# Expert routing weights spread over partitions by DMA instead of by TensorE

## The reference

```python
E, K = (16, 4); I_MOE, I_SH = (176, 704)
h = hidden_states.reshape(-1, 256)                  # 1024 tokens
probs = softmax(h @ router_w.T)                     # 16 experts
top_vals, top_idx = top_k(probs, K)
top_vals = top_vals / maximum(top_vals.sum(-1), 1e-9)
comb = zeros((N, E)).at[arange(N)[:, None], top_idx].add(top_vals)
g = einsum('nh,ehi->eni', h, w_gate)
u = einsum('nh,ehi->eni', h, w_up)
y = einsum('eni,eih->enh', silu(g) * u, w_down)
routed = einsum('enh,ne->nh', y, comb)
shared = silu(h @ sh_gate) * (h @ sh_up) @ sh_down
sg = sigmoid(h @ sh_gate_w)
return routed + sg * shared
```

## Time and profile before

| | |
|---|---|
| time, median of 3 runs | 1107.69 us (1105.7 to 1107.95) |
| profiled execution | 1106.63 us, of which the span from first to last instruction is 1104.8 |
| TensorE, matmul | 957.0 us busy, 87% |
| VectorE | 774.9 us, 70% |
| ScalarE | 644.1 us, 58% |
| GpSimd | 505.3 us, 46% |
| DMA | 43.12 MB moved |
| TensorE's clock, mean granted | 0.953 of full |
| share of the chain that ended last | TensorE 60%, VectorE 21%, ScalarE 8%, issue 8%, GpSimd 2% |

### The profile page before, as it was taken

How to read it: one execution, slowest core, us unless ns; L and a number is a source line. 1 busy time by engine, 2 the same in 40 slices (tenths; PEclk the granted TensorE clock), 3 DMA queues, 4 the chain that set the end, 5 groups by cost and what they waited for, 6 DMA issues and landing times.

```text
span 1104.8 us, 15499 instructions
## 1 busy us (share of the span) xinstructions
PE 957.0 (87%) x5250; PEld 597.8 (54%) x5250; DVE 774.9 (70%) x1292; ACT 644.1 (58%) x1517; POOL 505.3 (46%) x392
## 2 busy tenths in 40 slices
PE   5899797664767757789989999999999999999998
PEld 3666543241222225566667777777675655555555
DVE  4578789898999987788888777778875453233222
ACT  2655488888898628667886777777662332111110
POOL 3222364542878514787777566677554322000000
PEclk8899799896999988899999999999999999999999
DMA  9734014000000000000000620000040000000000
GB/s 334 300 132 153 1 45 134 2 1 0 1 0 0 1 0 1 1 1 2 1 1 1 186 75 3 2 1 1 1 134 1 1 1 1 1 20 1 0 1 20
DMA packets 24270, 43.12 MB, mean 39 GB/s; under 512 B 3648, under 2 KB 19968, under 8 KB 22656
## 3 DMA queue, kind: packets, MB, share of 16 engines
q1 hardware_dynamic: 24192, 42.14, 11.2%
HBM read 41.08 MB, written 1.05 MB: 38 GB/s over the span
## 4 chain that ended last, share of the span: by engine, by line
PE 60%; DVE 21%; ACT 8%; issue 8%; POOL 2%; DMA 0%; DVEq 0%; ACTq 0%; SPq 0%; POOLq 0%
PE ps L2336 14%; PE ps L2357 9%; PE ps L1908 4%; PE ps L1921 4%; DVE arena L1112 4%; PE ps L1867 4%; PE ps L1875 3%; DVE ps L1108 3%; ACT ps L2181 3%; PE ps L1892 3%; PE ps L1900 2%; PE ps L1882 2%; DVE arena L1117 2%; PE ps L2346 2%; PE ps L445 2%
## 5 line engine op out<-in xcount | busy, mean ns | idle before, releaser
L2375 DVE TENSOR_TENSOR arena<-arena,ps 128x512 f32<-128x512 f32 (+1 forms) x56 | 38.5, 688 | 145.9 <-ACT arena L2368 143.8
L2368 ACT ACTIVATE arena<-ps,arena 128x512 f32<-128x512 f32 (+1 forms) x56 | 38.4, 686 | 156.0 <-PE ps L2336 156.0
L2260 POOL TENSOR_TENSOR arena<-arena 128x4 f32<-128x4 f32 x96 | 98.8, 1029 | 50.1 <-DVE arena L2032 47.5
L2357 PE MATMUL ps<-wide,arena 128*128 128x256 f32 (+1 forms) x448 | 106.3, 380 | 0.0
L2181 ACT ACTIVATE ps<-ps,arena 128x128 f32<-128x128 f32 x256 | 88.4, 355 | 28.5 <-DVE arena L2011 28.5
L2173 ACT ACTIVATE arena<-ps,ones 128x512 f32<-128x512 f32 x96 | 68.1, 786 | 61.2 <-PE ps L1882 61.2
L2357 PEld LDWEIGHTS ps<-wide,arena 128*128 128x128 f32 (+1 forms) x448 | 84.7, 190 | 17.9 <-issue 1.8
L2336 PE MATMUL ps<-XT,wide 128*128 128x512 f16 (+1 forms) x384 | 93.3, 379 | 0.0
L2011 DVE TENSOR_REDUCE arena<-ps 128x4 f32<-128x512 f32 x64 | 43.7, 689 | 53.2 <-PE ps L1892 53.1
L1875 PE MATMUL ps<-wide,arena 128*128 128x512 f16 x256 | 67.1, 398 | 13.6 <-ACT arena L2173 7.1
L1112 DVE TENSOR_TENSOR_SCAN arena<-arena,ps 128x1024 f32<-128x1024 f32 x32 | 73.2, 2287 | 1.1
(11 more groups left out here) (343 smaller groups left out, 2321.7 us busy)
## 6 DMA issues: line engine op xcount, KB each, us to landing
side<-in_wproj SPq DMA_DIRECT2D x4, 1024.0 KB, 5.5
wide<-in_w_down SPq DMA_DIRECT2D x1, 3584.0 KB, 13.9
side<-in_w_gate SPq DMA_DIRECT2D x1, 3520.0 KB, 19.4
side<-in_w_up SPq DMA_DIRECT2D x1, 3520.0 KB, 12.2
wide<-in_w_gate SPq DMA_DIRECT2D x2, 1728.0 KB, 11.9
side<-in_w_up SPq DMA_DIRECT2D x3, 1024.0 KB, 9.2
arena<-in_taps SPq DMA_DIRECT2D x1, 2048.0 KB, 11.7
wide<-in_wq SPq DMA_DIRECT2D x1, 2048.0 KB, 18.0
```

The source lines that it names most:

```text
L2260: pool.tensor_tensor(rs[:, j, :], var[:, j, :], minus_half[:, j, :], ALU.pow).then_inc(rs_ready, 1)
L2357: last = pe.matmul(self.out(b), self.hid[n % 2][0:m, b * S:(b + 1) * S], self.down[0:m, j, :], start=(j == 0 and b % 2 == 0), stop=(j == M ...
```

## The change

The product that spreads the routing weights is gone, and with it `pick`, the f16 split and the factor 1024. In its place:

- `take_comb` copies the transposed routing weights, 17 x 512 in f32, from PSUM to SBUF (one VectorE operation where there were two).
- SP stores them to DRAM (`store_comb`) and loads them back as tiles (`load_weights`). For block j each expert that has columns in it gives one DMA, which reads that expert's row of 2 KB and repeats it over the expert's partitions. A block has one or two such DMAs. Three tiles in SBUF take turns; the load of tile n waits for the gating of tile n - 3.
- The gating reads the tile from SBUF, where it read PSUM. It waits for the load's semaphore.
- The first half's store and the loads of tiles 0 to 2 stand on SP's list ahead of the down weights. The second half's store stands ahead of tile 20's load. The stores of output batches 0 to 3 stand behind the load of tile 36.
- Two memsets and a small multiplication leave VectorE ahead of cross group 0, the factor 1024 leaves both routings, three operations leave GpSimd.

The diff, cut to its core:

```diff
-        self.pick = a.take([FM], F16)
-        self.combT = [a.take([4 * S], F16) for _ in range(2)]
+        self.combT = a.take([4 * S])
+        self.weights = [a.take([4 * S]) for _ in range(3)]
+        self.comb_rows = k.nc.dram_tensor("comb_rows", (2, E + 1, 4 * S), F32, kind="Internal").ap()
...
-    def place_pool(self, pool, i):
...
+    def store_comb(self, sp, h):
+        sp.wait_ge(self.combT_ready, 2 * h + 2)
+        sp.dma_start(self.comb_rows[h], self.combT[0:E + 1, :]).then_inc(self.comb_stored, 16)
+
+    def runs(self, j):
+        kind = [min(r // IM, E) for r in range(j * P, min((j + 1) * P, FM))]
+        return [(kind.index(e), kind.count(e), e) for e in sorted(set(kind))]
 
     def begin_vector(self, dve):
-        dve.memset(self.combT[0][0:49], 0.0)
-        dve.memset(self.combT[1][0:49], 0.0)
...
-        link(dve.tensor_tensor(self.comb[:, :, 0:E], self.left[:, :, 0:E],
-                               self.sums[:, 3, :].unsqueeze(2).broadcast_to([P, 4, E]), ALU.mult))
-        dve.tensor_scalar(self.comb, self.comb, self.COMB, None, ALU.mult).then_inc(self.combT_ready, 1)
+        dve.tensor_tensor(self.comb[:, :, 0:E], self.left[:, :, 0:E],
+                          self.sums[:, 3, :].unsqueeze(2).broadcast_to([P, 4, E]), ALU.mult).then_inc(self.combT_ready, 1)
...
-        link(dve.tensor_copy(hi, out[0:E + 1, :]))
-        dve.tensor_tensor(self.combT[h][32:32 + E + 1], out[0:E + 1, :], hi, ALU.subtract).then_inc(self.combT_ready, 1)
+        wait(dve, self.comb_stored, 16 * h)
+        dve.tensor_copy(self.combT[0:E + 1, :], out[0:E + 1, :]).then_inc(self.combT_ready, 1)
...
         moe.load(sp, 2)
+        moe.store_comb(sp, 0)
+        for n in range(3):
+            k.blocks.load_weights(sp, n)
         sp.wait_ge(proj_psum, 4 * NG)
         moe.load_down(sp)
...
-    def spread(self, pe, n):
...
+    def load_weights(self, sp, n):
+        h, j = self.order[n]
         if j == 0:
-            pe.wait_ge(moe.combT_ready, 2 * h + 2)
-            pe.wait_ge(moe.pick_ready, 3)
-        wait(pe, self.gated_ready, n)
-        pe.matmul(self.ps[0:m, self.COMB_BANK, :], moe.pick[0:49, j * P:j * P + m], moe.combT[h][0:49], start=True,
-                  stop=True).then_inc(self.comb_psum, 1)
+            sp.wait_ge(self.moe.comb_stored, 16 * (h + 1))
+        wait(sp, self.gated_ready, n - 2)
+        for first, rows, e in self.moe.runs(j):
+            sp.dma_start(self.moe.weights[n % 3][first:first + rows, :],
+                         self.moe.comb_rows[h, e:e + 1, :].broadcast_to([rows, 4 * S])
+                         ).then_inc(self.moe.weights_loaded[n % 3], 16)
...
         dve.wait_ge(self.silu_ready, n + 1)
-        dve.wait_ge(self.comb_psum, n + 1)
-        dve.tensor_tensor(self.gated[n % 2][0:m], self.silu[n % 2][0:m], self.ps[0:m, self.COMB_BANK, :],
+        dve.wait_ge(self.moe.weights_loaded[n % 3], self.weights_count(n))
+        dve.tensor_tensor(self.gated[n % 2][0:m], self.silu[n % 2][0:m], self.moe.weights[n % 3][0:m],
                           ALU.mult).then_inc(self.gated_ready, 1)
...
+    def sync(sp):
+        for n in range(3, N):
+            if n == 20:
+                moe.store_comb(sp, 1)
+            blocks.load_weights(sp, n)
+            if n == MC + 8:
+                for b in range(4):
+                    k.store(sp, b)
```

More of the change, by code:

```diff
@@ L2478, in _ @@
                     part["sync"](sp)
-            for b in range(B):
-                sp.wait_ge(k.batch_done, b + 1)
-                sp.dma_start(out[b], k.X[:, b, :]).then_inc(stored, 16)
-            sp.wait_ge(stored, 16 * B)
+            for b in range(4, B):
+                k.store(sp, b)
+            sp.wait_ge(k.stored, 16 * B)
         @block.vector
```

50 lines of the change are left out of this document (16 added, 34 removed).

## The result

The changed kernel takes 1076.0 us (median of 4 runs, 1071.4 to 1077.2) beside 1107.1 for the kernel before on the same chip: ratio 0.9713, 95% interval 0.9682 to 0.9743.

The account below looks back on a forecast made before the run. TensorE was taken to bound the expert stage, waits between engines the cross stage. Seven terms summed to 28.9 us off 1106.63, so 1077.7, or 1079 against the runs' median; range 1076 to 1085.

Parts of the forecast that it names:

- Regular tiles: Expert stage, tiles 4 to 55: each falls from 4.74 to 4.32 us without the spread, 21.8 us gained.
- Rival 3: Expert stage: the up block keeps its extra 0.11 us behind a gate block, 5.7 us less gained, 1084.5; chance 0.05.
- Large cast, small cast, memsets: Cross stage: dropping GpSimd's casts gains 2.8 us in groups 3 and 4, 0.5 in 5 and 6; dropping memsets 0.5.
- Rival 2: Cross stage: VectorE's waits form again beside another GpSimd operation, 5.7 us less gained, 1084.5; chance 0.09.
- Scaling: End of the first half's routing: dropping the multiplication by 1024 and its meeting with GpSimd gains 1.9 us.
- Entry: Tiles 0 to 3: down 2 starts at 845.0 in place of 846.67, 1.7 us gained (0.6 to 1.9).
- rival 1: Before down 0: the down weights, behind store and loads on SP's queue, land 1 to 3 us late, 1080 to 1082; chance 0.17.
- The gating from SBUF: VectorE's gating in each tile: takes 0.69 us as from PSUM; 0.2 charged at the entry for meeting GpSimd.
- Routing of the second half: Transposes after tile 14: routing needs 10.6 us from up 12's end, TensorE arrives after 10.4; cost 0.3 us.
- Loads of weights: DMA queues, expert stage: a tile's load takes about 3 us of 12.3 available, so it is hidden.
- Rival 4: Expert stage: every gating waits for its load, 5.6 us a tile at 16 us landings, 1144 in all; chance 0.03.
- rival 5: More than the sum: the entry's gap closes further or more GpSimd meetings fall away, 1075 to 1077; chance 0.10.

Follow-up runs that it names:

- again2: The changed kernel unaltered, timed a further time beside the kernel before: 1075.9 us, ratio 0.9716.
- again: The changed kernel unaltered, timed once more beside the kernel before: 1078.1 us, ratio 0.9746.
- spread49: The changed kernel plus one unread 49-row product between gate and up products in each of the 56 tiles: 1097.9 us, ratio 0.9918.
- casts: The changed kernel with GpSimd's two casts put back in cross groups 3 and 5, writing where nothing reads: 1080.5 us, ratio 0.9761.
- scaling: The changed kernel with the last operation of both routings put back, as a multiplication by 1.0: 1078.4 us, ratio 0.9749.
- down_first: The changed kernel with the down weights' load issued right behind the store of the routing weights, ahead of tile loads: 1075.9 us, ratio 0.9723.
- turn_later: The changed kernel with the second half's routing transposes behind tile 15, not 14, and their copy behind gating 16: 1078.3 us, ratio 0.9742.

## Why the prediction was wrong, and where it was right

The step that failed is the starting point. The forecast took 1106.63, one execution of before, and subtracted seven terms of the change from it; all that lies ahead of the cross stage was put at nothing, as if it were the same in both kernels, and no reason was given. It was 6.7 us shorter in the profiled execution by 400 us, and the average executions of the two kernels differ by some 2 us more than the terms. Why is open: the traces show the granted clock that goes with it, not what sets the clock. How narrowly the range was missed is chance: by the ratio of again2 the time would be 1076.2, by that of again 1079.6, and both lie inside.

- **Regular tiles** (21.8): right, 22.1. A tile is 4.32 us, and spread49 restores the whole of it. Rival 3 (the up block keeps its 0.11) is out. What the 0.11 was, a change of shape, I did not see.
- **Large cast, small cast, memsets** (2.8, 0.5, 0.5): right to 0.05 in the profiled execution, and casts returns the first two. The memsets are the soft one, 0.15 to 0.5 over the fifteen traces. Comparing like groups in the same trace was a sound way. Rival 2 is out.
- **Scaling** (1.9): 2.1 in the changed kernel's trace and in scaling's.
- **Entry** (1.7): the step that failed within the sum; it gave 0.66. The cause is the down weights, which I had left at no charge and as rival 1. The store took 2.85 us to the first load for my 1.8, the five issues 2.24 for 2.0, and the down weights 15.5 to land for 13.9: 2.9 us later than reckoned, beyond the 2.4 of slack. That cost 0.89. With down_first the entry gives 1.55 of the 1.7. The meeting with GpSimd that I charged 0.2 for cost 0.1 there (gating 2 took 0.78 for 0.70).
- **The gating from SBUF**: I took 0.69, as from PSUM. That is so in nineteen of the 28 tiles of the first half; nine gatings took 0.77 to 1.76 us. Timelines of GpSimd and VectorE for one of them:

```profile
833.70 1.16 POOL L1583 TENSOR_TENSOR wide<-XN,wide 128x512 f16<-128x512 f32 x1 [1.01 <-ACT wide L1576]
```

```profile
834.24 1.16 DVE L2373 TENSOR_TENSOR arena<-arena 128x512 f32<-128x512 f32 x1 [1.27 <-ACT arena L2366]
```

  It starts while GpSimd is at work, and ends 0.54 behind it. From tile 3 to tile 5 the gatings are 3.7 us apart, below 4.32, so it cost nothing, as forecast. The Trainium skill's rule quoted ahead (SBUF — State Buffer, section "Who interferes with whom") agrees.
- **Routing of the second half** (-0.3): 0.51 of idle time, 0.69 by turn_later. The place of the wait was right, and its size 0.4 short. Half of that is in what the routing hangs on. I had it start from the end of up 12. VectorE's timelines at gating and weighing of tile 12, before and then after:

```profile
891.87 0.75 DVE L2383 SCALAR_TENSOR_TENSOR arena<-ps,arena 128x512 f32<-128x512 f32 x1 [0.32 <-PE ps L2336]
```

```profile
873.64 0.69 DVE L2373 TENSOR_TENSOR arena<-arena 128x512 f32<-128x512 f32 x1 [1.76 <-ACT arena L2366]
874.42 0.75 DVE L2381 SCALAR_TENSOR_TENSOR arena<-ps,arena 128x512 f32<-128x512 f32 x1
```

  Before, the weighing waited for up 12 and started 0.04 us behind its end (891.83 in the chain). Now up 12 comes closer behind gate 12 and is through first (its six products run from 872.71 for 1.46 us, to 874.17), and the weighing starts 0.25 behind it, when its gating is done. So the change moved the chain onto the SiLU and the gating, 0.2 us later. The other 0.2 is that a stop costs TensorE somewhat more than its idle time, as at down 0.
- **Loads of weights** (hidden): right, with three tiles and even with one. Rival 4 is out by a wide margin; its formula is wrong for a wait that other idle time absorbs.
- **The sum** was right: 28.2 for 28.9. From the profiled execution of before that is 1078.4 us. In part its errors cancel: entry and routing gave 1.4 less, the other rows 0.7 more.
- **The range and the chances** failed. They were made of the terms alone. What lies ahead of 400 us was 1 us behind to 7 ahead in single traces and 1.7 ahead in the mean. The lower end stood 3 us below the forecast and should have stood 6 or 7; rival 5 (more than the sum) was given 0.10 for mechanisms of the change, and came about through none of them.

## What to carry to other kernels

Ask of a product with few rows among products of 128 rows what it costs beside them. Here 80 and 128 rows cost 0.2 us and 49 rows twice that; where between 49 and 80 the step lies was not timed (64 rows show the same idle time of the weight loader as 49). Rows of zeros made the product cheaper; setting them to zero cost 2.5 us once. When a step is put on a DMA queue, work out how much later everything behind it is issued and lands, with times of transfers of the same shape. And when a change is worth a few per cent, let the range of the forecast take in how much the stages scatter that the change doesn't touch.

## What the runs showed of the hardware

- A product of 49 rows by 512 columns in f16 between products of 128 rows costs 0.43 us; of 80 or 128 rows 0.20 to 0.22; a second of 49 rows beside the first 0.22. Worked out from these, each change of shape is 0.11.
- A VectorE operation on 68 elements a partition took 0.20 us in the second half's routing, and 2.06 where it started 0.11 behind a GpSimd operation of 2.12.
- A store of 17 rows of 2 KB took 2.85 us from issue to the next instruction behind its landing; 16 rows and 1 row as two stores 2.22.
- One row of DRAM repeated over up to 128 partitions, 256 KB, lands in 3.1 us (1.8 to 4.6 over all 84 loads), while TensorE is full and keeps its pace to 0.01 us.
- The same early code got the lower clock level in three quarters, two fifths or none of an 18 us stretch, and took 4.5, 2.0 or 0 us more.
